# A five-place weight ring, and a second attention block whose next q, k, v and combinations are issued earlier

## The chip, the cores and the metric

One core of one Trainium2 chip (trn2) runs the whole kernel in one launch. The metric is the device time of an execution in microseconds. Engines are named TensorE (PE; PEld its weight loads), VectorE (DVE), ScalarE (ACT), GpSimd (POOL) and SyncE (SP, which issues most transfers).

## The reference, cut to what matters

Eight images of 16 x 16 tokens with 192 channels go through two blocks, each an attention and a mixture of experts (MoE). The norms are layer norms without weights, except `rms_norm`.

```
x = x + neighbourhood_attention(ln(x))            # 12 heads of 16, 7 x 7 neighbours
t = t + moe0(ln(t))                               # 32 experts of width 464, each token to 6,
                                                  # at most 48 tokens an expert; shared part of width 928
x = x + window_attention(ln(x))                   # within each row of 16 tokens
def L1_ffn(u):                                    # u = ln(t)
    h = u + causal_attention(rms_norm(u) @ w_qkv) # 12 query, 3 key heads, rotary, 256 tokens an image
    m = rms_norm(h)
    return h + sum_of_2_of_16_experts(m)          # width 384
t = t + L1_ffn(ln(t))
```

The output is x after both blocks, 2048 tokens by 192.

## The kernel before, in words

The kernel keeps x in SBUF (`x_all`, two tiles of 128 tokens an image). Five engines run their own instruction streams, which meet in semaphores. Matmul results go to eight PSUM banks, S0, S1, T0, T1, O0, O1, M0, M1. There are five stages.

*Stage A* is a loop over the images: neighbourhood attention, routing of the first MoE and its shared part. The tokens' normalised rows go to DRAM (`rows0`); `onehot` and small matmuls (`slot_ids`) count which token fills which place of an expert. Every image also has SyncE fill an eighth of the DRAM table `sorted_x` with an empty row (line 858). At the end of image 7, `a_tail` (line 1177) waits for the shared part, adds it to x, adds the ids, and only then line 1269 casts them to integers for the gathers.

*Stage B* runs the 32 experts as 16 pairs, of 64 slots each, two pairs a turn, in eight turns. GpSimd gathers the rows of the 16 pairs by indirect DMA (line 949) and copies two pairs at a time into `xs` (`b_x`, line 953; ScalarE copies the first two); TensorE transposes them (`b_rows`, lines 717 and 719), multiplies by gate and up weights (`b_gate_up`, lines 1690 and 1695), transposes the product, and multiplies by the down weights (line 1718); VectorE weighs the output (line 1292) and splits it into three bf16 parts, `y0_all`, whose sum is the f32 value. Weights of two pairs have a place (`RING = 2`); a refill waits for `b_gu` (gate and up used) or `b_y` (down used).

*Stage C*, the second block, combines the experts' outputs: for an image, `c_onehot` on GpSimd makes 32 bf16 matrices of 128 x 128 (`comb_s`, line 972), and TensorE multiplies them with `y0_all` (`c_comb`, line 1736) for each tile of tokens in a bank of its own. Its prologue combines image 0 and runs its window attention; then a loop over the images (`c_body`) does: add the window projection to x; normalise (statistics on VectorE, inverse root on GpSimd, lines 923 and 924, apply at line 809); root mean square norm (squares on ScalarE, another root on GpSimd); transposes (line 730); causal q, k, v (line 1761); rotation and the split into bf16 parts (`split_qk`); transposes of q and k (line 509); causal attention; projection (line 615); the second norm into `m_row`; then the window attention of the *next* image, with the router's steps of this one between its groups. The next image's combination is in two halves, one for each tile of tokens, one at the turn's start and one behind the causal q, k, v; its normalising and its q, k, v (`next_qkv`, lines 744 and 751) stand between the first two groups of scores of causal attention.

Attention works in groups `u`: scores (a mask matmul, line 535, then the heads, line 538) into a score bank; VectorE the negated maximum (line 651); ScalarE the exponentials (line 680); TensorE transposes of the probabilities (line 555); VectorE and ScalarE in turn the copies (lines 624 and 689); TensorE the weighting of v (line 573), `late` groups behind; at the end denominators (line 581), division on VectorE (641, 642), transposes (603), a copy (695) and the projection (615). `extra`, `between` and `before` are tables of steps which other parts of the kernel put between the groups. Each engine's order is the order written, so whatever stands in such a table delays what is behind it on that engine.

*Stage D* sorts tokens by expert into 48 tiles and runs the second MoE (`f_` functions, lines 1811 to 1837) with weights in a ring of six; the last stage adds its rows to x.

## Time and profile before

| | us |
|---|---|
| median of 3 runs | 1372.81 (1372.27 to 1373.34) |
| the profiled execution | 1371.57 |
| its span, first to last instruction | 1369.7 |
| TensorE busy in the span | 1081.2 (79%) |
| VectorE busy | 756.1 (55%) |
| ScalarE busy | 488.2 (36%) |
| GpSimd busy | 351.6 (26%) |
| mean granted clock of TensorE | 0.91 of full |

Busy time is a share of the whole span; no engine is busy throughout, and each stage has a limit of its own. A timeline row gives start and length in us, engine, line, what it writes and reads, how many instructions it merges, and in brackets the engine's idle time before it and who ended it.

### The profile page before, as it was taken

The numbers are of one execution on the slowest core, as the hardware profiler recorded it, in microseconds if no ns is written. First come the engines' busy times: TensorE is split into PE (matmuls) and PEld (weight loads), VectorE is DVE, ScalarE is ACT, GpSimd is POOL, SyncE is SP. The second block draws the span as 40 slices with busy tenths as digits, with TensorE's granted clock in tenths as the row PEclk, the third lists the DMA queues.
The fourth block names the chain that finished last, engine by engine and source line by source line (L and its number), as shares of the span: only waits on it lengthen the run. The fifth ranks groups of instructions, "written<-read, shape, count | busy, mean of one in ns | idle before, by whom it ended". The sixth has DMA issues, their size and how long they took to land.

```text
span 1369.7 us, 27161 instructions
## 1 busy us (share of the span) xinstructions
PE 1081.2 (79%) x9278; PEld 811.8 (59%) x9317; DVE 756.1 (55%) x2331; ACT 488.2 (36%) x1212; POOL 351.6 (26%) x588
## 2 busy tenths in 40 slices
PE   4899999999984997687777777777777662989993
PEld 3677777667762444455555556555555442878883
DVE  6668667766740343466665666666656553232324
ACT  2355345335521231435352534343444440211210
POOL 0000000000004024552533425161616101223332
PEclk9999999999986999799988999999989775999997
DMA  9054224404437793000000000000000003788885
GB/s 339 2 131 130 65 65 130 127 12 121 130 110 187 283 396 144 0 17 1 15 0 15 0 15 0 15 0 15 0 15 0 10 7 116 273 279 276 310 290 177
DMA packets 69193, 144.58 MB, mean 106 GB/s; under 512 B 4961, under 2 KB 55425, under 8 KB 66849
## 3 DMA queue, kind: packets, MB, share of 16 engines
q1 hardware_dynamic: 64352, 132.76, 29.3%
q0 software_dynamic: 4800, 11.32, 2.6%
q8 instruction: 22, 0.36, 0.1%
q14 instruction: 19, 0.15, 0.0%
HBM read 97.22 MB, written 46.83 MB: 105 GB/s over the span
## 4 chain that ended last, share of the span: by engine, by line
PE 34%; issue 33%; DVE 15%; POOL 8%; ACT 6%; DMA 4%; POOLq 0%; DVEq 0%; ACTq 0%; SPq 0%
PE bank L1607 4%; PE bank L1736 3%; PE bank L555 3%; PE bank L615 3%; PE bank L1635 3%; PE bank L573 3%; DMA R<-in_ffn_gu 2%; PE bank L1761 2%; PE bank L744 2%; DVE neg_max L651 2%; POOL rstd L924 2%; PE bank L751 2%; POOL R L972 2%; DVE R L624 1%; POOL token_y L1016 1%
## 5 line engine op out<-in xcount | busy, mean ns | idle before, releaser
L680 ACT ACTIVATE R<-bank,neg_max 128x128 f32<-128x128 f32 (+2 forms) x576 | 186.7, 405 | 91.3 <-DVE neg_max L651 90.6
L972 POOL TENSOR_SCALAR R<-cf,ids_rel 128x128 bf16<-128x128 f32 x288 | 187.9, 668 | 0.1
L923 POOL TENSOR_TENSOR rstd<-mean_var,cf 128x2 f32<-128x2 f32 x32 | 6.2, 193 | 625.0 <-DVE mean_var L804 625.0
L651 DVE TENSOR_REDUCE neg_max<-bank 128x2 f32<-128x352 f32 (+2 forms) x216 | 129.8, 611 | 47.0 <-PE bank L538 38.7
L555 PE MATMUL bank<-cf,R 128*128 128x128 f32 x864 | 135.2, 280 | 23.6 <-ACT R L689 17.5
L555 PEld LDWEIGHTS bank<-cf,R 128*128 128x128 f32 x864 | 94.8, 142 | 40.7 <-ACT R L689 16.2
L702 ACT ACTIVATE R<-bank 128x1024 bf16<-128x1024 bf16 x72 | 69.4, 1017 | 110.3 <-PE bank L509 110.3
L1607 PE MATMUL bank<-R 64*116 64x256 f32 (+1 forms) x512 | 97.4, 398 | 0.0
L509 PE MATMUL bank<-cb,R 128*128 128x128 bf16 x1008 | 74.6, 245 | 20.7 <-DVE R L494 20.4
L1522 DVE TENSOR_TENSOR R<-R,bank 128x384 f32<-128x384 f32 x48 | 26.6, 554 | 115.2 <-ACT R L1112 112.6
L1821 PE MATMUL bank<-xsT,R 128*128 128x128 f32 x576 | 76.3, 286 | 17.0 <-DMA R<-in_ffn_w 15.7
L509 PEld LDWEIGHTS bank<-cb,R 128*128 128x128 bf16 x1008 | 71.4, 113 | 27.8 <-DVE R L494 18.2
L538 PE MATMUL bank<-R 128*128 128x128 bf16 (+2 forms) x576 | 76.5, 235 | 11.5 <-DVE R L711 5.2
L1821 PEld LDWEIGHTS bank<-xsT,R 128*128 128x128 f32 x576 | 70.4, 197 | 23.6 <-DMA R<-in_ffn_w 15.0
L1607 PEld LDWEIGHTS bank<-R 64*116 64x116 f32 (+1 forms) x512 | 65.2, 180 | 26.2 <-issue 16.4
L1736 PE MATMUL bank<-R 128*128 128x384 bf16 (+1 forms) x512 | 74.6, 311 | 2.6 <-DVE R L1301 2.6
L1112 ACT ACTIVATE R<-bank 128x384 f32<-128x384 f32 x48 | 23.5, 490 | 148.4 <-PE bank L1828 148.4
L535 PE MATMUL bank<-cb 128*128 128x352 bf16 (+1 forms) x177 | 61.7, 349 | 14.8 <-ACT R L702 8.6
L689 ACT ACTIVATE R<-bank 128x512 f32<-128x512 f32 (+2 forms) x152 | 64.2, 460 | 14.7 <-PE bank L555 14.7
L1736 PEld LDWEIGHTS bank<-R 128*128 128x128 bf16 x512 | 51.8, 107 | 26.7 <-issue 8.7
L538 PEld LDWEIGHTS bank<-R 128*128 128x128 bf16 x576 | 50.5, 98 | 22.9 <-issue 0.5
L573 PE MATMUL bank<-R 128*32 128x128 f32 x1152 | 50.2, 281 | 14.8 <-ACT R L689 14.8
(249 smaller groups left out, 2006.2 us busy)
## 6 DMA issues: line engine op xcount, KB each, us to landing
R<-in_ffn_w SPq DMA_DIRECT2D x48, 864.0 KB, 6.1
sorted_x<-cmp SPq DMA_DIRECT2D x8, 4128.0 KB, 16.8
R<-in_ffn_gu SPq DMA_DIRECT2D x16, 1392.0 KB, 7.9
R<-in_ffn_dn SPq DMA_DIRECT2D x16, 768.0 KB, 5.8
xs_words<-sorted_x SPq DMA_DIRECT2D x48, 129.0 KB, 2.8
R<-token_y SPq DMA_DIRECT2D x8, 384.0 KB, 6.3
rows<-R SPq DMA_DIRECT2D x8, 224.0 KB, 2.3
out_x<-x_all SPq DMA_DIRECT2D x16, 96.0 KB, 2.5
```

The source lines that it names most:

```text
L509: ins = nc.tensor.transpose(bank[:, :].bitcast(BF16)[:, (h * 2 + t) * P:(h * 2 + t + 1) * P], qk_parts[:, row, :, :].rearrange("p s e -> p ...
L538: ins = nc.tensor.matmul(bank[:, g * kw:(g + 1) * kw], q_ap(h, t), k_ap(a, h, k0, kw), start=False, stop=(g == len(heads) - 1))
L555: ins = nc.tensor.transpose(PT[u % 2][:, at + g * P:at + (g + 1) * P], probs[:, u % 3, g * kw + c0:g * kw + c0 + P], ident)
L573: ins = nc.tensor.matmul(OB[t][j * HV:(j + 1) * HV, col:col + P], v_ap(a, h, vt), probsT[:, u % 4, at + g * P:at + (g + 1) * P], start=(k ...
L651: nc.vector.tensor_reduce(neg_max[:, u % 4, 0:g], score_bank(a, u)[:, 0:g * kw].rearrange("p (g k) -> p g k", g=g), AX, ALU.max, negate=Tr ...
L680: ins = nc.scalar.activation(probs[:, u % 3, g * kw:(g + 1) * kw], score_bank(a, u)[:, g * kw:(g + 1) * kw], ACT.Exp, bias=neg_max[:, u % ...
L689: copies_pt(lambda dst, src: nc.scalar.activation(dst, src, ACT.Copy), a, v).then_inc(psem("pta"), 1)
L702: nc.scalar.activation(qkT[:, h0:h0 + heads, :].rearrange("p h t -> p (h t)"), bank[:, :].bitcast(BF16)[:, 0:heads * 256], ACT.Copy, scale ...
L972: ins = nc.gpsimd.tensor_scalar(comb_s[:, t, j, :], cst("iota_tok"), ids_rel[:, j:j + 1], None, ALU.is_equal)
L1607: ins = nc.tensor.matmul(GATE[g % 3][part][0:DP0, c * 256:(c + 1) * 256], wsgu[rows, 2 if k else part, at:at + DP0], xnT_all[rows, k, :], ...
L1736: ins = nc.tensor.matmul(COMB[t][:, 0:(k1 - k0) * C], comb_s[:, t, j, :], y0_all[:, j, k0:k1, :].rearrange("p s c -> p (s c)"), start=(j = ...
L1821: nc.tensor.matmul(GU[r][part][:, c * P:(c + 1) * P], w[:, part * FF + c * P:part * FF + (c + 1) * P], xsT[:, r, 0, :], start=(c == 0), st ...
```

## The change

It has four parts. (1) The ring of stage B has five places, laid over buffers that stage A has done with; each place is loaded when what lay there is released; each later refill waits for the same semaphores as before, five pairs on. Gathered rows are read where they land, each two pairs have a semaphore (`b_rows0` to `b_rows7`), the loops of B are written out, and image 7's ids are added before its shared part (which goes to M0). (2) In stage C the combination of image i + 2 is in M1 alone, in three matmuls of 192 columns a step, 8 of 32 steps at the start of turn i and 24 behind the causal q, k, v; images 0 and 1 are combined before the loop. (3) The next image's normalised rows are transposed in the previous window attention, and its q, k, v are multiplied right behind the window projection; VectorE reads them before it applies the norm. (4) All attentions use three score banks; logits and ranks lie elsewhere. In stage D four of the first row loads move behind weight loads.

```
-RING = 2
+RING = 5
...
-        PT, OB, COMB = [T0, T1], [O0, O1], [T0, M1]
-        def score_banks(a):
-            return [S0, S1, M0] if a is NEIGH else [S0, S1, M0, M1]
+        LOGITS = M1[:, 2 * C:2 * C + 2 * E1]
+        SCORE = [S0, S1, M0]
...
-                if u == 3 and routed is not None:
-                    pe.wait_ge(s("c_expl"), routed)
...
-                    if u == min(us[-1] + late, a.n + 2):
+                    if u == min(us[-1] + 2 + len(us), a.n + 2):
...
+            for j, ready in ((2, lambda: await_(sp, NEIGH, "proj", B - 1, 1)), (3, lambda: sp.wait_ge(s("a_h"), GP * B)),
+                             (4, lambda: sp.wait_ge(s("a_shared"), B))):
+                ready()
+                load_gate_up(j)
+                load_down(j)
+            for j0 in range(RING, NPAIR, 2):
+                last = min(j0 + 2, NPAIR)
+                for j in range(j0, last):
+                    sp.wait_ge(s(f"b_gu{(j - RING) % 2}"), 2 * ((j - RING) // 2) + 2)
+                    load_gate_up(j)
+                for j in range(j0, last):
+                    sp.wait_ge(s("b_y"), (j - RING) // 2 + 1)
+                    load_down(j)
...
-            for t in range(WRING):
+            for t in (0, 1):
                 load_rows(t, t)
-            for t in range(1, WRING):
+            for t in (1, 2):
+                load_weights(t, t)
...
-                    .then_inc(s("b_rows_first" if j < 2 else "b_rows_rest"), 16)
-            pool.wait_ge(s("b_rows_rest"), 16 * (NPAIR - 2))
-            with pool.Fori(1, NPAIR // 2) as jj:
-                pool.wait_ge(s("b_xT"), jj)
-                b_x(jj)
+                    .then_inc(s(f"b_rows{j // 2}"), 16)
+            pool.wait_ge(s("a_done"), B + 1)
...
+            for i in range(3):
+                if i:
+                    pool.wait_ge(s("c_comb"), 2 * i)
+                    c_root(link, "c_var", i, mv, EPS6)
                 for t in range(2):
+                    c_onehot(link, i, t)
...
                 c_scatter(i)
-                if more:
-                    pool.wait_ge(s("c_comb"), 2 * i + 4)
-                    c_root(link, "c_var", 2 * i + 3, mv, EPS6)
-                    c_onehot(link, i + 2)
+                if level == 2:
+                    c_root(link, "c_var", 2 * i + 4, mv, EPS6)
+                    pool.wait_ge(s("c_comb"), 2 * i + 6)
+                    c_onehot(link, i + 3, 0)
                 c_root(link, "c_ss", 2 * i + 2, ss, EPS6)
+                if level == 2:
+                    c_onehot(link, i + 3, 1)
...
                 ln_stats(link, i, s("c_var"))
-                dve.wait_ge(s("c_rstd"), 4 * i + 2)
+                if level:
+                    conv_qk_dve(dve, WINDOW, brow, i + 1)
+                dve.wait_ge(s("c_rstd"), 4 * i + (3 - short(i)))
                 link(ln_apply(u_sb, i))
...
-                if more:
-                    c_combine(link, i + 1)
                 run(qk_copies_dve(dve, CAUSAL, i))
+                if level:
+                    between.update(zip(range(2, 8), split_qk(WINDOW, i + 1, link)))
+                if level == 2:
+                    between[1] = lambda: c_combine(link, i + 2)
+                    between[8] = lambda: c_norm(i + 2, 4 * i + 5)
...
+            def c_comb(i, n0, n1):
+                for n in range(n0, n1):
+                    t, j = divmod(n, NPAIR)
+                    if j == 0:
+                        pe.wait_ge(s("c_onehot"), 2 * i + t + 1)
+                    for k in range(3):
+                        ins = nc.tensor.matmul(M1[:, t * C:(t + 1) * C], comb_s[:, t, j, :], y0_all[:, j, k, :],
+                                               start=(j == 0 and k == 0), stop=(j == NPAIR - 1 and k == 2))
...
+            attention_pe(pe, WINDOW, 0, {2: lambda: c_comb(1, 0, 2 * NPAIR), (WINDOW.n, "transposed"): lambda: c_head(2)})
...
+                if level:
+                    pe.wait_ge(s("c_slots"), i + 1)
+                    pe.wait_ge(s("c_xTc"), 3 * i + 2)
+                    conv_qk_pe(pe, WINDOW, headT, wqkv, i + 1)
+                    conv_v_pe(pe, WINDOW, headT, wqkv, i + 1)
+                if level == 2:
+                    c_comb(i + 2, 0, EARLY_COMB)
+                c_head(2 * i + (3 - short(i)), M0)
...
+                if level == 2:
+                    c_comb(i + 2, EARLY_COMB, 2 * NPAIR)
                 transpose_qk(pe, CAUSAL, i)
-                attention_pe(pe, CAUSAL, i, None, {1: next_qkv, 2: banks_read} if more else {})
+                attention_pe(pe, CAUSAL, i, {"weighted": lambda: transpose_qk(pe, WINDOW, i + 1, n1=4)} if level else {})
                 project(pe, CAUSAL, wof, i)
-                if more:
-                    transpose_qk(pe, WINDOW, i + 1)
+                if level:
+                    transpose_qk(pe, WINDOW, i + 1, n0=4)
```

`level` is 2 for images 0 to 5, 1 for image 6 and 0 for image 7. On VectorE two of the window copies (`qk_copies_dve`) run before the causal projection is awaited; on ScalarE one does, and the copy of the next image's transposed rows (`c_copy` into `headT`) is put before the last gathering of outputs. `EARLY_COMB` is 8. The window projection goes to T0 and the causal one to M0. The loads of stage C's weights stand behind the ring's loads.

## Rows read from the trace of the kernel before

**Rows 1.** The page's first line

```profile
span 1369.7 us, 27161 instructions
```

**Rows 2.** Timeline of VectorE, 408 to 418 us

```profile
407.97 0.69 DVE L1242 TENSOR_TENSOR R<-R,bank 116x512 f32<-116x512 f32 x1 [0.61 <-ACT R L1042]
...
416.37 0.56 DVE L1180 TENSOR_TENSOR x_all<-x_all,bank 128x384 f32<-128x384 f32 x1 [7.42 <-PE bank L1635]
...
417.70 0.17 DVE L1269 CAST ids_i<-ids_f 128x16 int32<-128x16 f32 x1
```

**Rows 3.** Timeline of TensorE, 424 to 447 us

```profile
424.39 0.45 PE L717 MATMUL bank<-cf,xs_words 128*128 128x128 f32 x1 [8.13 <-ACT xs_words L1055]
...
433.36 1.01 PE L1695 MATMUL bank<-R,xsT 64*64 64x464 f32 x8
446.67 0.48 PE L717 MATMUL bank<-cf,xs_words 128*128 128x128 f32 x1 [12.30 <-POOL xs_words L955]
```

**Rows 4.** Source view of line 1292: min/median/max ns, first and last start

```profile
L1292 DVE TENSOR_TENSOR y_f<-bank,wsl x8: 557/558/559, 453.9 to 530.1; 128x384 f32<-128x384 f32 x8
```

**Rows 5.** Windows view: busy us of PE to POOL, granted clock, DMA share, GB/s

```profile
456.00:524.00 68.00, 63.67 (x504) 32.00 (x500) 28.57 (x59) 20.67 (x30) 20.90 (x37) 1.00 0.99 402
```

**Rows 6.** Source view of line 1338, the first VectorE step of a turn

```profile
L1338 DVE TENSOR_TENSOR x_all<-x_all,bank x8: 553/554/556, 583.4 to 1085.8; 128x384 f32 x7, 128x384 f32<-128x384 f32 x1
```

**Rows 7.** Timeline of one turn of stage C, all engines

```profile
870.57 4.09 PE L1736 MATMUL bank<-R 128*128 128x384 bf16 x32
870.88 0.55 DVE L1338 TENSOR_TENSOR x_all<-x_all,bank 128x384 f32 x1 [1.50 <-PE bank L615]
...
873.45 0.67 DVE L809 TENSOR_SCALAR h_words<-x_all,mean_var,rstd 128x192 f32 x2 [1.08 <-POOL rstd L924]
...
876.96 0.68 PE L730 MATMUL bank<-cf,R 128*96 128x128 f32 x4 [2.31 <-DVE R L1349]
...
878.33 4.21 PE L1761 MATMUL bank<-wqkvf,R 96*128 96x288 f32 x8 [0.68 <-ACT R L735]
...
882.33 5.34 PE L1736 MATMUL bank<-R 128*128 128x384 bf16 x32
...
887.75 1.85 PE L509 MATMUL bank<-cb,R 128*128 128x128 bf16 x30
...
893.49 2.84 PE L744 MATMUL bank<-wqkv,R 96*128 96x384 f32 x8 [0.76 <-ACT R L735]
...
898.21 0.68 DVE L651 TENSOR_REDUCE neg_max<-bank 128x4 f32<-128x512 f32 x1
```

**Rows 8.** Windows view of the same turn's causal q, k, v

```profile
877.00:882.30 5.30, 4.62 (x12) 3.08 (x13) 1.54 (x7) 0.59 (x1) 3.42 (x4) 0.60 0.27 100
```

**Rows 9.** Timeline of TensorE, the end of causal attention

```profile
912.64 0.65 PE L573 MATMUL bank<-R,v_causal 128*32 128x128 f32 x16 [0.87 <-DVE R L624]
...
916.31 2.93 PE L615 MATMUL bank<-wof,R 96*128 96x192 f32 x8 [0.68 <-ACT R L695]
919.03 4.47 PE L509 MATMUL bank<-cb,R 128*128 128x128 bf16 x48
...
924.02 0.39 PE L538 MATMUL bank<-R 128*128 128x128 bf16 x4
```

**Rows 10.** Source view of line 949, gathers issued at 418 to 421 us

```profile
DMA to landing us min/median/max: 3.8/4.1/5.1
```

**Rows 11.** The same, gathers issued at 432 to 437 us

```profile
DMA to landing us min/median/max: 8.5/8.6/9.2
```

**Rows 12.** Source view of line 858 at 398.3 us, the last fill

```profile
DMA to landing us min/median/max: 16.6/16.6/16.6
```

**Rows 13.** Timeline of TensorE in the first window attention

```profile
568.28 0.66 PE L555 MATMUL bank<-cf,R 128*128 128x128 f32 x4 [1.64 <-ACT R L680]
```

**Rows 14.** Source view of line 972, image 1's one-hots on GpSimd

```profile
L972 POOL TENSOR_SCALAR R<-cf,ids_rel x32: 593/597/1717, 546.0 to 567.4; 128x128 bf16<-128x128 f32 x32
```

**Rows 15.** Timeline of TensorE at the start of stage D

```profile
1162.79 2.93 PE L1821 MATMUL bank<-xsT,R 128*128 128x128 f32 x12 [2.92 <-DMA R<-in_ffn_w]
```

More of the change, by code:

```diff
@@ L399, in build @@
             psem(n)
+        for n in ("qkv", "read"):
+            psem(n, CAUSAL)
         block = ctx.enter_context(nc.Block())
@@ L781, in turns, with turns_c, short @@
             body(n - 1, False)
+        def turns_c(eng, body):
+            with eng.Fori(0, B - 2) as i:
+                body(i, 2)
+            body(B - 2, 1)
+            body(B - 1, 0)
+        def short(i):
+            return 1 if isinstance(i, int) and i == B - 1 else 0
         def tile_x(i, t):
@@ L1065, in b_body, with c_copy, c_body @@
                 nc.scalar.activation(hTs[0:DP0, 0, :], PT[0][0:DP0, :], ACT.Copy).then_inc(s("b_hTc0"), 1)
-            turns(act, NPAIR // 2, b_body)
-            def c_copy(k):
+            for jj in range(NPAIR // 2):
+                b_body(jj, jj + 1 < NPAIR // 2)
+            def c_copy(k, dst=xnT, bank=M0):
                 act.wait_ge(s("c_xT"), k)
-                copy_pair(xnT).then_inc(s("c_xTc"), 1)
-            c_copy(1)
+                copy_pair(dst, bank).then_inc(s("c_xTc"), 1)
+            c_copy(1, headT, S0)
             run(qk_copies_act(act, WINDOW, 0))
-            attention_act(act, WINDOW, 0)
-            def c_body(i, more):
+            attention_act(act, WINDOW, 0, last=lambda: c_copy(2, headT, S0))
+            def c_body(i, level):
                 def squares(n):
@@ L1082, in squares @@
                     ins.then_inc(s("c_ss"), 1)
+                steps = qk_copies_act(act, WINDOW, i + 1) if level else []
                 squares(0)
-                c_copy(3 * i + 2)
+                c_copy(3 * i + (3 - short(i)))
                 run(qk_copies_act(act, CAUSAL, i))
-                attention_act(act, CAUSAL, i, {0: lambda: c_copy(3 * i + 3)} if more else {})
+                attention_act(act, CAUSAL, i)
+                run(steps[:1])
                 squares(1)
+                run(steps[1:2])
+                c_copy(3 * i + (4 - short(i)))
+                run(steps[2:])
                 def router():
@@ L1256, in a_body @@
                     link(nc.vector.tensor_tensor(before0[:, :], before0[:, :], mask_b[:, t, :], ALU.add))
-                if not more:
-                    a_tail(link, i)
-                elif not first:
+                if more and not first:
                     link.end()
@@ L1380, in c_body @@
-                if more:
-                    steps += split_qk(WINDOW, i + 1, link)
-                attention_dve(dve, CAUSAL, i, link, dict(zip(range(1, 9), steps)) if more else {})
+                between = {}
+                if level:
[3 more added lines that the diff above has]
+                    between[8] = lambda: c_norm(i + 2, 4 * i + 5)
+                attention_dve(dve, CAUSAL, i, link, between)
@@ L1384, in c_body @@
+                copies = qk_copies_dve(dve, WINDOW, i + 1) if level else []
+                run(copies[:2])
                 await_(dve, CAUSAL, "proj", i, 1)
-                link(nc.vector.tensor_tensor(u_sb[:, :, :], u_sb[:, :, :], two(M1[:, 0:2 * C]), ALU.add))
+                link(nc.vector.tensor_tensor(u_sb[:, :, :], u_sb[:, :, :], two(M0[:, 0:2 * C]), ALU.add))
                 nc.vector.memset(scratch[:, 13:14], 0.0).then_inc(s("c_u"), 1)
-                link(nc.vector.tensor_tensor(image_x(i), image_x(i), two(M1[:, 0:2 * C]), ALU.add))
@@ L1388, in c_body @@
-                if more:
-                    copies = qk_copies_dve(dve, WINDOW, i + 1)
-                    run(copies[:1])
+                link(nc.vector.tensor_tensor(image_x(i), image_x(i), two(M0[:, 0:2 * C]), ALU.add))
                 dve.wait_ge(s("scattered"), 64 * i + 64)
                 nc.vector.tensor_scalar(m_row[:, :, TOKC], m_row[:, :, TOKC], 2.0 * P, None, ALU.add)
-                rms(1, m_row, 4 * i + (5 if more else 4)).then_inc(s("c_mr"), 1)
-                if more:
-                    run(copies[1:])
+                rms(1, m_row, 4 * i + (6 - (level < 2) - short(i))).then_inc(s("c_mr"), 1)
@@ L1398, in highest_logit @@
+                run(copies[2:])
                 def highest_logit():
                     dve.wait_ge(s("c_logits"), i + 1)
[L1400 removed]
+                    nc.vector.tensor_reduce(wsum[:, :, 0], two(LOGITS), AX, ALU.max, negate=True)\
                         .then_inc(s("c_negmax"), 1)
@@ L1724, in b_body @@
                     b_gate_up(jj + 1)
-            turns(pe, NPAIR // 2, b_body)
+            for jj in range(NPAIR // 2):
+                b_body(jj, jj + 1 < NPAIR // 2)
             pe.wait_ge(s("b_done"), LINKS["B"] * (NPAIR // 2))
```

342 lines of the change are left out of this document (177 added, 165 removed).

## The prediction

> **What bounds the kernel now.** I read the page first, for the span, which the sum below is made against [rows 1]; then busy time by stretch; then, because no engine is busy throughout, the timelines of four places, each from the last instruction backwards to what it waited for.
>
> *The hand-over to the first experts.* VectorE ends its part of image 7 at 408.7 us, but slot numbers are cast only at 417.7, behind the 6.9 us shared down-projection [rows 2]. TensorE's first expert transpose is at 424.4 and its second at 446.7, after 12.3 us of idle [rows 3]: GpSimd copies no later pair before all 14 later gathers have landed (line 956). The first pair's output is read at 453.9, the eighth's at 530.1 [rows 4].
>
> *The expert stream.* From 456 to 524 us the DMA engines are 99% busy at 402 GB/s [rows 5]. A pair of experts is 2.21 MB, 5.5 us, so a turn of two costs 11.0; observed are (530.1 - 453.9)/7 = 10.9. Both the transfers and TensorE's chain are at that length.
>
> *The second block (stage C).* Seven turns from 583.4 to 1085.8 us, 71.8 each [rows 6]. In the turn from 870.88 [rows 7] the start is a chain of small steps (add, statistics, root, apply), during which TensorE combines half of the next image in 4.09 us and then idles 2.3 us until 876.96. Its clock then falls: the eight q, k, v matmuls of 288 columns take 4.21 us, and the granted clock is 0.60 there [rows 8]; eight of 384 columns take 2.84 at 893.49. From 887.75 to 916.31 is causal attention. From 898.21 to 912.6 VectorE works almost without a break and TensorE's last weighting waits for it [rows 7, 9]. So VectorE sets the length there, and the preparation of the next image at 891 to 897 (attention stands still) is paid in full.
>
> **The change, part by part.**
>
> *Earlier gathers.* ids are added before the shared down-projection ends: cast at about 409.7, 8 us sooner. A gather lands after 3.8 to 5.1 us alone and 8.5 to 9.2 beside weight loads [rows 10, 11]. The last zero fill, issued at 398.3, flies for 16.6 us, to 414.9 [rows 12], and the new loads of experts 2 and 3 stand behind it, so I take the long landing: the second gather, issued at 411.4, is there at 420. TensorE needs its down-projection (to 416.3) and x added (417.0) first, so it starts at 420 in place of 424.4; 417 is the lower bound. "Trainium Kernel Development and Optimization", Key Constraints, in the Trainium skill says that DMAs issued by SyncE and GpSimd run on the same 16 engines and interleave; the trace agrees, by those two landings.
>
> *One wait per pair, and rows read in place.* From the first transpose to the end of gate and up were 10.0 us (424.39 to 434.37), from the second transpose to the output's read 7.2 (446.67 to 453.9) [rows 3, 4]. With the 12.3 us of idle gone the first output is read at 420 + 10 + 7.2, less 1 us for ScalarE's copy of rows: 436, instead of 453.9.
>
> *Ring of five.* Experts 2, 3 and 4 are asked for at 399, 409 and 416 us, when image 7's row, gating and shared part release their places, and from then on the ring runs a turn and a half ahead, so no turn waits for a single refill. With 7 more turns of 10.9 the eighth is read at 512. The stream allows about 508: 14 pairs at 5.5 us from 415, with some 10 us for the gathers (my estimate, from their landings while little else was in flight), is 502, and about 6 of work after the last weights. I take 511, a gain of 19; bounds 24 (start at 417, all cover holds) and 10 (each refill late). The unrolled loops add no work of an engine. The three weight loads for the second block move behind the ring, to about 500, and are hidden until 511.
>
> *Before the second block's loop.* The first combination has 96 matmuls of 192 columns instead of 64 of 384 and 192. The columns are the same; a step of 576 took 4.09/16 = 0.256 us [rows 7]. "TensorE: Matmul & The Clock Gate", Back-to-back issue gap, in the Trainium skill gives 81 ns for matmuls of 128 columns and 131 ns for 512 in a stream with weight loads, so three short ones would cost more than a long and a short one: interpolated, an estimate of 0.27 against 0.20 us, 2 us more an image. The trace does not agree: its 0.256 is already what the columns take at 2.4 GHz (0.240) plus little. I take no change; by the page it would be 16 us more over all images. The second image's combination is now inside the first window attention: 32 x 0.256 = 8.2 us, of which the 1.6 us that TensorE waited there (568.28) are cover [rows 13]. With its VectorE step +8.
>
> *One root behind 32 one-hots.* GpSimd makes image 2's one-hots before the loop, and only after image 1's combination is added. Image 1's took 22 us (546.0 to 568) [rows 14]. The combination's end is C; VectorE adds it at C + 4, the root follows, the one-hots run from C + 6.5 to C + 28.5. The rest of attention is 583.4 - 568.3 = 15.1 [rows 6, 13] plus 1, so turn 0 wants its own root at C + 17.5 and gets it at C + 29.5 where it could use it at C + 19.5: 10 us. Everything of the turn stands behind that root. In later turns one half of 16 runs under attention and one after the second root, with 7 us or more to spare.
>
> *A steady turn.* (a) Start: VectorE reads two banks of q and k before it applies the first root. The second is ready 2.84 us after TensorE begins, so the apply moves from 2.57 to 3.45: +0.9. TensorE meanwhile does 4.3 us of q, k, v (V is half of 2.84) and 8 combination steps (2.0), which end before x is normalised at 7.0. The idle time is filled, so I take the full clock: 288 columns then cost 2.1 in place of 4.21, -2.1. Behind them stand 24 steps, 6.1 us, against VectorE's 7.1 us of rotation and splitting from the first bank: both end at 16.6 to 16.9; before, 16.87. So 0. (b) Causal attention: the maximum of group 2 began 10.5 us after the transposes (898.21); with no preparation between, it can after two copies, two maxima and the combination's add and statistics (1.5), at 5.6: -4.9. The 14.4 us behind it stay and get 0.7 for normalising and some gaps: -3.8. (c) 32 of 48 transposes move ahead of the last denominators, at 62 ns (30 in 1.85) to 93 ns (48 in 4.47), less 0.6 of idle there: +1.9. (d) The projection took 2.93 us, half speed by the row of 384 columns; perhaps full: -0.7. (e) Before scores stood 48 transposes and those of m_row, 4.8 us after the projection (924.02); now 16 stand, but m_row is due at 3.5 by the same chain of add, squares, root and apply as at the turn's start, less the statistics, so scores gain 0.6, exponentials, which lose two ScalarE copies before them, 1.2, and group 3 waits no more for the router: -1.5. Sum -4.1; bounds -5.5 and +3 (half clock in a). Three banks in place of four cost nothing: scores of group u wait for the exponentials of u - 3, for which TensorE's preceding transposes have already waited.
>
> *Seven turns*: turn 0 has -4 + 10 and, after 10 us idle, half clock: +9.5. Five turns -20. Turn 6 has no combination or normalising: -5. The last turn 0.
>
> *Stage D*: TensorE waited 2.9 us for the second weights at 1162.79 [rows 15]; issued four row loads earlier, they are there: -3.5 with the clock's gain.
>
> Sum: -19 + 8 + 9.5 - 20 - 5 - 3.5 = -30. The profiled execution took 1371.57 us (1369.7 of span and 1.9 around it), 1.2 below the median of three, so 1342 to 1343; I say 1342.
>
> **Rivals.** (1) *Clock as before*: q, k, v keep 4.21 us and end at 12.5. The second group of 16 steps took 5.34 us where the first took 4.09, so 5.6 of them ran at half rate (0.48 us a step); with as many again, 24 steps end at 19.9, not 16.9: +3 in six turns, 1360. For it: this turn and its clock [rows 8]. Against: TensorE had idled 2.3 us before the fall, and the change fills that. 0.15. (2) *Slower*: TensorE stays at half clock until the combination is through. Steps of 0.48 us, 24 of them behind 4.2, end at 24.1: +7.2 in six turns, 1385. It decides from 22.0 us of the turn on, where six turns lose the 31 us. Against it: in that second group the clock came back. 0.06. (3) *The ring brings little*: gathers and refills hold the stream up, the eighth output is at 521: 1352. 0.09. (4) *More*: attention in (b) ends as VectorE's work alone, (c) is hidden by a full clock, the root stall is 5 us: -2 in six turns and -5, 1325. 0.12. (5) The stated case, 1330 to 1354 by its own terms: 0.58.
>
> **Numbers.** A measurement of this kernel tells about 0.2%, 2.7 us. Slower is (2) but for its milder end: 0.05; within 0.2% are that end and the tail of (1) near 1370: 0.03; faster the rest: 0.92. Range 1320 to 1364: it takes in (1), (3), most of (4).
>
> **What would show it.** First output near 436 and eighth near 511; turn 0 with a wait of about 10 us for a root behind one-hots; later turns of 67 to 68 us; granted clock 1.0 at the causal q, k, v, in about 2.1 us; transposes of causal attention 17 us into the turn; no wait for the second weights in stage D. I would be wrong if the combination's three pieces cost more than their columns, or if TensorE's clock does not hold.

## The result, and the profile after

The changed kernel took 1319.76 us in the median of four runs (1314.41 to 1323.49), the kernel before beside it 1373.07 (1372.27 to 1373.38): a ratio of 0.961, with a 95% interval of 0.9585 to 0.9639. It is faster, by 53 us where 30 were forecast, and 0.24 us below the low end of the range. Later runs of it gave 1315.87 (0.958) and 1316.05 (0.959). The profiled execution took 1314.41, 5.35 under the median, so the stage times below add up to a little more than the median's gain.

Where the 57.1 us between the two profiled spans are, in us:

| part | before | after | change | forecast |
|---|---|---|---|---|
| start to the eighth expert output | 530.1 | 511.7 | -18.4 | -19 |
| from there to the first turn | 53.3 | 58.1 | +4.8 | +8 |
| turn 0 | 69.9 | 74.9 | +5.0 | +9.5 against the mean turn of 71.8, so 81.3 |
| turns 1 to 5 | 360.9 | 324.0 | -36.9 | -20 |
| turn 6 | 71.6 | 65.0 | -6.6 | -5 |
| turn 7 and stage D | 283.9 | 278.9 | -5.0 | -3.5 |

(Turn 1 of the kernel before is a long one, 75.9 us; against its mean turn of 71.8 turns 1 to 5 gained 35.0.)

The page's first line, and the source views of the line that reads an expert output and of the first VectorE step of a turn; they answer to [rows 1, 4, 6]:

```profile
span 1312.6 us, 27217 instructions
```

```profile
L1341 DVE TENSOR_TENSOR y_f<-bank,wsl x8: 557/558/559, 436.1 to 511.7; 128x384 f32<-128x384 f32 x8
...
L1388 DVE TENSOR_TENSOR x_all<-x_all,bank x8: 553/554/555, 569.8 to 1033.7; 128x384 f32 x6, 128x384 f32<-128x384 f32 x2
```

TensorE's first expert transpose (timeline; it answers to [rows 3]) waits for the second gather and starts at 420.5, the forecast's 420; the first output is at 436, the eighth at 512, both as forecast.

```profile
420.53 0.44 PE L739 MATMUL bank<-cf,R 128*128 128x128 f32 x1 [6.47 <-DMA R<-rows,ids_i]
```

TensorE's timeline of the turn that starts at 839.10, against [rows 7, 9]:

```profile
842.67 2.15 PE L1796 MATMUL bank<-R 128*128 128x192 bf16 x24
845.54 0.68 PE L752 MATMUL bank<-cf,R 128*96 128x128 f32 x4 [0.73 <-DVE R L1401]
846.91 2.21 PE L1826 MATMUL bank<-wqkvf,R 96*128 96x288 f32 x8 [0.68 <-ACT R L757]
848.95 6.11 PE L1796 MATMUL bank<-R 128*128 128x192 bf16 x72
...
875.44 1.96 PE L536 MATMUL bank<-cb,R 128*128 128x128 bf16 x32
...
879.61 1.57 PE L637 MATMUL bank<-wof,R 96*128 96x192 f32 x8 [0.68 <-ACT R L717]
881.01 1.06 PE L536 MATMUL bank<-cb,R 128*128 128x128 bf16 x16
884.75 1.10 PE L752 MATMUL bank<-cf,m_row 128*96 128x128 f32 x4 [2.68 <-DVE m_row L1401]
```

The causal q, k, v take 2.21 us, not 4.21; a combination step costs 6.11/24 = 0.255 us, as its columns; and the projection takes 1.57 us, not 2.93. The windows view shows the granted clock, of a turn of before and of two of after (columns as in [rows 5]):

```profile
870.90:942.60 71.70, 54.52 (x467) 39.65 (x471) 45.26 (x144) 30.43 (x82) 29.46 (x49) 0.90 0.02 7
```

```profile
839.10:904.00 64.90, 49.54 (x498) 38.36 (x501) 44.17 (x140) 30.59 (x82) 29.53 (x49) 0.97 0.02 8
968.70:1033.70 65.00, 43.63 (x397) 31.37 (x400) 41.69 (x131) 30.07 (x81) 6.87 (x11) 0.92 0.03 9
```

A granted clock of 0.50 is TensorE at 1.2 GHz (half clock below), 1.00 is 2.4 GHz. The turn of before has 13.7 us at half clock, in two stretches of 6.8 us of which these windows show most:

```profile
878.00:884.60 6.60, 6.27 (x18) 4.12 (x19) 3.47 (x15) 0.27 (x1) 2.73 (x3) 0.50 0.22 80
915.60:922.30 6.70, 6.02 (x40) 5.82 (x40) 2.21 (x7) 2.30 (x6) 0.91 (x2) 0.50 0.00 0
```

The first takes in the causal q, k, v, the second the projection and the 48 transposes behind it [rows 7, 9]. After, 3.4 us are left (884.7 to 888.1). Work on VectorE, ScalarE and GpSimd is the same to about 1 us. Turn 0 has its wait of 7.8 us for a root, and the one-hots before it took 18.9 us in place of the 22 of [rows 14] (timeline of VectorE):

```profile
581.20 0.67 DVE L845 TENSOR_SCALAR h_words<-x_all,mean_var,rstd 128x192 f32 x2 [7.77 <-POOL rstd L971]
```

### The profile page after: what moved, and what is told of

Read it like the earlier page. It is cut to its first block, busy times and chain, and to the rows that moved or that the text cites. A ratio compares the mean times of both kernels' runs of the same rounds, so it can differ in the third digit from the quotient of the medians.

```text
span 1312.6 us, 27217 instructions
## 1 busy us (share of the span) xinstructions
PE 1043.5 (80%) x9541; PEld 805.9 (61%) x9573; DVE 747.4 (57%) x2308; ACT 481.1 (37%) x1205; POOL 347.6 (26%) x581
## 4 chain that ended last, share of the span: by engine, by line
issue 33%; PE 27%; POOL 17%; DVE 12%; ACT 5%; DMA 5%; POOLq 1%; DVEq 0%; ACTq 0%; SPq 0%
POOL R L1010 10%; PE bank L1659 4%; DMA R<-in_ffn_gu 3%; PE bank L577 2%; PE bank L1687 2%; POOL rstd L971 2%; POOL sorted_x L1031 2%; PE bank L595 2%; DVE neg_max L673 2%; PE bank L637 2%; POOL token_y L1058 1%; ACT R L702 1%; PE bank L1796 1%; PE bank L536 1%; PE bank L1746 1%
## 5 line engine op out<-in xcount | busy, mean ns | idle before, releaser
L1882 PE MATMUL bank<-xsT,R 128*128 128x128 f32 x576 | 75.9, 285 | 13.1 <-DMA R<-in_ffn_w 11.4
L536 PE MATMUL bank<-cb,R 128*128 128x128 bf16 x1008 | 67.5, 230 | 21.8 <-DVE R L521 21.8
L560 PE MATMUL bank<-R 128*128 128x128 bf16 (+2 forms) x576 | 79.4, 243 | 5.3 <-issue 4.6
L536 PEld LDWEIGHTS bank<-cb,R 128*128 128x128 bf16 x1008 | 62.8, 104 | 28.7 <-DVE R L521 17.9
L1154 ACT ACTIVATE R<-bank 128x384 f32<-128x384 f32 x48 | 23.6, 491 | 142.6 <-PE bank L1889 142.6
L557 PE MATMUL bank<-cb 128*128 128x352 bf16 (+1 forms) x184 | 65.8, 357 | 3.6 <-ACT R L724 3.2
L1796 PE MATMUL bank<-R 128*128 128x192 bf16 x768 | 66.0, 247 | 2.6 <-DVE R L1350 2.6
L560 PEld LDWEIGHTS bank<-R 128*128 128x128 bf16 x576 | 53.0, 103 | 24.6 <-issue 3.6
L1796 PEld LDWEIGHTS bank<-R 128*128 128x128 bf16 x768 | 64.1, 98 | 4.9 <-DVE R L1350 3.0
```

The costliest lines, as they stand in the source:

```text
L536: ins = nc.tensor.transpose(bank[:, :].bitcast(BF16)[:, (h * 2 + t) * P:(h * 2 + t + 1) * P], qk_parts[:, row, :, :].rearrange("p s e -> p ...
L557: nc.tensor.matmul(bank[:, 0:len(heads) * kw], cstb("identb"), cstb(mname, moff, len(heads) * kw), start=True, stop=False)
L560: ins = nc.tensor.matmul(bank[:, g * kw:(g + 1) * kw], q_ap(h, t), k_ap(a, h, k0, kw), start=False, stop=(g == len(heads) - 1))
L1796: ins = nc.tensor.matmul(M1[:, t * C:(t + 1) * C], comb_s[:, t, j, :], y0_all[:, j, k, :], start=(j == 0 and k == 0), stop=(j == NPAIR - 1 ...
L1882: nc.tensor.matmul(GU[r][part][:, c * P:(c + 1) * P], w[:, part * FF + c * P:part * FF + (c + 1) * P], xsT[:, r, 0, :], start=(c == 0), st ...
```

## The experiments

The question was why a steady turn fell by 6.8 us (71.7 to 64.9) and not by 4.1. Theory A: a good part is TensorE's clock, far beyond the causal q, k, v for which the prediction counted it. Theory B: the order of the work alone. Edits are to the changed kernel unless said otherwise.

### The changed kernel again (two runs)

> The changed kernel once more, nothing edited. Its four times went from 1314.41 to 1323.49 us at mean granted clocks of 0.940 to 0.929, while four of the kernel before kept within 1.1 us. If the 9 us come from the place of half-clock stretches, the times spread over 1314 to 1324 again, the longer ones at the lower clock, and the profile differs from the first one in a few turns by 1 to 2 us each where the granted clock is low. If they come from transfers (rival), the difference stands in the first block, in the expert stages or in stage D (before 511.7 or after 1096.8 us) at the same clock. If it was chance of one chip (rival), all times agree within 1.5 us.

> The changed kernel, nothing edited, beside the other three. Its turns took 64.9 us in both profiles (3.4 us of half clock in each) and its times 1313.9 to 1323.5. If the times spread by the turns' clock, a longer execution shows turns above 64.9; if the spread stands in turn 0, turn 7 and stage D alone (rival), the steady turns are 64.9 again whatever the time. 1314 to 1323.

1315.87 us (1313.87 to 1316.86) and 1316.05 (1315.35 to 1319.17). The steady turns are 64.9 again in both profiles, with 3.4 us of half clock each; turn 0 took 75.3 and 74.7 and began at 572.1 and 572.7 (569.8 in the first), turn 7 and stage D together took 275.3 and 277.7 (278.9 in the first). So the spread is not in the steady turns; what of it could be profiled stands ahead of turn 0 and behind turn 6. No execution of 1323 us was profiled, so its cause stays open.

### The combination late

```
-EARLY_COMB = 8
+EARLY_COMB = 0
```

> All 32 steps of the combination behind the causal projection of a turn, none ahead of the transposes of its input. If columns are what counts and the 8 early steps fill a wait of TensorE, 8 steps of 0.255 us go onto the path: +2.0 us in each of the six turns with a combination, +12 us in all. If the early steps also hold the clock (rival), TensorE idles 2.9 us at the turn's start, the causal projection runs at 4.2 instead of 2.2 us and the steps behind it at half clock for a while: +4 to +6 us a turn, +24 to +36 us. If the attention behind it has slack on TensorE (rival), 0 to +0.5 us a turn.

1358.61 us (1350.24 to 1360.46), +43 against the changed kernel beside it: more than any case expected. TensorE's timeline and the window of one turn:

```profile
874.51 0.68 PE L752 MATMUL bank<-cf,R 128*96 128x128 f32 x4 [2.71 <-DVE R L1401]
875.88 3.65 PE L1824 MATMUL bank<-wqkvf,R 96*128 96x288 f32 x8 [0.68 <-ACT R L757]
879.31 8.37 PE L1796 MATMUL bank<-R 128*128 128x192 bf16 x96
```

```profile
866.20:937.90 71.70, 55.20 (x502) 41.72 (x502) 44.23 (x140) 30.56 (x82) 29.44 (x49) 0.90 0.02 7
```

With 2.7 us of idle at that place the turn is as long as before the change, and has the same 13.7 us at half clock. Two microseconds of work, moved, are worth the whole gain of a steady turn. That can be the clock or the order, hence the next run.

### Idle products in the place of the early steps

```
-EARLY_COMB = 8
+EARLY_COMB = 0
 ...
+for n in range(24):
+    nc.tensor.matmul(M1[:, 0:C], cstb("identb"), y0_all[:, n % NPAIR, 0, :], start=True, stop=True)
-c_comb(i + 2, 0, EARLY_COMB)
```

> As the run with the combination late (none of its 32 steps ahead of the transposes), but 24 products of 192 columns whose sum nobody reads stand in the place of its first 8 steps. A steady turn took 71.7 us with the combination late and 64.9 with 8 steps early. If TensorE's work at that place counts only because it keeps the clock up, a turn needs the 2.0 us of 8 steps more than the changed kernel and nothing else: 66.9 us, the causal projection at 2.2 us, 13 to 15 us more than the changed kernel in all (1328 to 1333). If it is the order of the real work that counts (rival), the products only add to the path: 71.7 us or more, 1358 and above.

1336.68 us (1336.02 to 1337.96). Turns of 67.7 to 68.6, so products whose sum nobody reads give back 3.1 to 4.0 of the 6.8 us. In the turn from 717.7 the transposes of causal q and k begin 1.9 us later than in the changed kernel (17.8 against 15.85 us into the turn): the eight steps, as theory A has it. It ends 3.7 later all the same, with half clock in its last 21 us (765.7 to 773, and from 783 on). The time lies 4 us above theory A's 1328 to 1333 and far from theory B's 1358, so the clock is the larger part and idle products hold it less well than early steps.

```profile
717.70:786.40 68.70, 55.21 (x526) 42.99 (x525) 44.24 (x141) 30.56 (x82) 29.45 (x49) 0.93 0.02 8
```

### One piece of the combination

Only the largest of the three bf16 pieces of the expert outputs is combined; the two smaller ones are left out.

```
-for k in range(3):
+for k in range(1):
```

> The combination multiplies only the first of the three pieces of the expert outputs (the two smaller ones are left out, so the sum is rounded to bf16): 32 products of 192 columns in place of 96, 5.4 us of TensorE less for each image at full clock. If the 24 steps behind the projection lie on the path of a steady turn, a turn gets 6.1 - 2.0 = 4.1 us shorter: -25 us in turns and -5 us in the head. If TensorE's busy time there is also what keeps the clock up (rival), the granted clock of the steady turns falls from 0.97 to about 0.90, and the transposes, scores and copies that follow take most of it back: 0 to -1.5 us a turn. If VectorE's rotary and split set the transposes' start (rival: the split ends at 854.89, the combination at 855.06, 0.2 us apart), a turn gains 0.2 us only and the whole -3 to -6 us, most of it in the head.

1319.82 us (1318.85 to 1320.87), 4 us more than the changed kernel, though each image has 5.4 us less work on TensorE. From the eighth expert output to turn 0 it takes 8 to 10 us less; the turns are longer:

```profile
634.90:700.10 65.20, 47.40 (x438) 34.44 (x437) 44.15 (x141) 30.39 (x82) 29.46 (x49) 0.95 0.02 8
700.10:768.50 68.40, 51.17 (x439) 38.04 (x438) 44.29 (x141) 30.88 (x82) 29.44 (x49) 0.88 0.02 8
```

Causal q, k, v are back at 4.2 us in both, and the transposes start at 17.2. VectorE's split now ends last there: TensorE waits 1.8 and 2.1 us for it. So in these turns the combination's 6 us are not on the path: they lie beside VectorE's work, and they hold the clock.

### The kernel before with idle products

```
 if more:
     c_comb(i + 1, 0)
+for n in range(24):
+    nc.tensor.matmul(S1[:, 0:C], cstb("identb"), y0_all[:, n % NPAIR, 0, :], start=True, stop=True)
```

> The kernel before, with 24 products of 192 columns that nobody reads put ahead of the transposes of the causal input in each turn, where TensorE waited 2.31 us for VectorE and the clock then was at half for 6.8 us. If work at that place keeps the clock up, the causal projection takes 2.2 instead of 4.2 us and the second half of the combination 4.1 instead of 5.3: 2.5 to 3.5 us a turn, eight turns, 1345 to 1353 us without any of the change; the clock would then be the better part of what the change gains in a steady turn. If the clock falls because of the low rate of the whole turn, not of this wait (rival), 0 to -0.5 us a turn: 1369 to 1373. If the products push the transposes (rival: they start 2.3 us before rms ends and take 2.0 to 4.0), 0 to +1.5 us a turn, up to 1385.

1365.66 us (1357.06 to 1374.27), a ratio of 0.992 (0.989 to 0.995): faster than before by adding work. Windows of four successive turns of one execution:

```profile
803.60:871.70 68.10, 51.20 (x496) 37.10 (x495) 45.02 (x144) 30.48 (x82) 29.48 (x49) 1.00 0.02 8
871.70:939.70 68.00, 51.24 (x495) 37.06 (x493) 44.93 (x144) 30.52 (x82) 29.77 (x49) 1.00 0.02 8
939.70:1011.30 71.60, 55.84 (x496) 40.37 (x494) 44.99 (x143) 30.59 (x82) 29.48 (x49) 0.90 0.02 7
1011.30:1085.30 74.00, 58.51 (x495) 42.07 (x493) 44.98 (x144) 30.65 (x82) 29.76 (x49) 0.85 0.02 7
```

The code of the turns is one loop, and VectorE, ScalarE and GpSimd are busy for the same time in each; only the clock differs. At full clock the old order takes 68.0 us (TensorE still waits 0.32 us behind the products, so they put nothing on its path). In that turn's timeline the old projection and transposes are at full speed too:

```profile
877.74 0.69 PE L730 MATMUL bank<-cf,R 128*96 128x128 f32 x4 [0.32 <-DVE R L1349]
879.10 2.21 PE L1763 MATMUL bank<-wqkvf,R 96*128 96x288 f32 x8 [0.68 <-ACT R L735]
...
915.31 1.57 PE L615 MATMUL bank<-wof,R 96*128 96x192 f32 x8 [0.68 <-ACT R L695]
916.71 2.85 PE L509 MATMUL bank<-cb,R 128*128 128x128 bf16 x48
920.40 0.68 PE L730 MATMUL bank<-cf,m_row 128*96 128x128 f32 x4 [0.84 <-DVE m_row L1349]
```

Against [rows 7, 9]: 2.21 for 4.21, 1.57 for 2.93, 2.85 for 4.47. With 32 products instead of 24:

> The kernel before with 32 idle products in place of 24 ahead of the causal input's transposes. With 24, three turns kept full clock at 68.0 us, the others took 71.7 to 73.9, and the times went from 1357 to 1374. If the share of the clock in a steady turn of the kernel before is 3.7 us, turns 2 to 6 take 68.0 to 68.7 (the 8 further products push the transposes by up to 0.7 us) and the whole 1350 to 1358. If 24 were already too many or the place is the wrong one for the other stretch (rival), the turns stay mixed: 1357 to 1374, as with 24.

1366.59 us (1356.94 to 1372.1): turns of 68.1 to 74.3 in one profile, mixed as with 24. One filled place does not secure the clock in the old order; where it holds, the turn is at 68 to 69.

### The transposes behind the projection

```
-attention_pe(pe, CAUSAL, i, {"weighted": lambda: transpose_qk(pe, WINDOW, i + 1, n1=4)} if level else {})
+attention_pe(pe, CAUSAL, i)
 project(pe, CAUSAL, wof, i)
-    transpose_qk(pe, WINDOW, i + 1, n0=4)
+    transpose_qk(pe, WINDOW, i + 1)
```

and their copies on ScalarE and VectorE behind the second squares and the second rms.

> The 32 transposes of the next image's q and k that stand ahead of the causal denominators go behind the projection, to the 16 that are there, and their copies on ScalarE and VectorE behind the second squares and the second rms. If they cost on the path what they take (1.96 us from 875.44 to 877.40), the projection comes 2.0 us earlier; the 48 transposes then take 3.2 us and end about as m_row is ready (PE waited 2.68 us there), so TensorE loses nothing, but the score products wait for the copies, which now end 1.5 to 2.5 us later: a turn changes by -0.5 to +1.0 us, the whole by -4 to +7. If the first products of the next attention hang on the copies alone (rival), +2.5 us a turn, +17. If the copies overlap the router's start (rival), -2 us a turn, -14. The half-clock stretch at 884.7 (3.4 us) should go where TensorE no longer idles there.

1335.55 us (1324.15 to 1340.31), +20, though in the profiled execution some turns are shorter than the changed kernel's 64.9:

```profile
648.50:716.80 68.30, 55.66 (x502) 42.74 (x502) 44.30 (x140) 30.55 (x82) 29.46 (x49) 0.90 0.02 8
785.10:851.00 65.90, 52.93 (x502) 39.46 (x502) 44.14 (x141) 30.60 (x82) 29.47 (x49) 0.95 0.02 8
851.00:914.80 63.80, 51.10 (x502) 38.84 (x501) 43.95 (x140) 30.60 (x82) 29.53 (x49) 0.97 0.02 8
```

At an equal clock of 0.97 the turn is 1.1 us shorter without the 32 transposes ahead of the denominators. Three of its five steady turns were at 65.8 or 68.3.

### Sixteen steps early, alone and with the transposes behind

> 16 in place of 8 of the combination's 32 steps ahead of the transposes. TensorE waited 0.73 us there in the changed kernel, so 8 more steps (2.0 us) push the transposes by 1.3 us and free 2.0 us behind the projection, where the combination and VectorE's split ended within 0.2 us of each other: the split, which starts from the projection, would now end 1.3 us later: +1.3 us in six turns, +8 us. If the combination's end is the bound (rival), -0.7 us a turn, -4 us. If the clock is now less at risk (rival), the times spread less, within 2 us, at +0 to +8.

`EARLY_COMB = 16`: 1317.07 us (1314.37 to 1320.55), no difference from 8. A steady turn has no half clock left and is as long as before:

```profile
841.90:906.80 64.90, 49.16 (x502) 37.34 (x501) 44.10 (x140) 30.44 (x82) 29.48 (x49) 1.00 0.02 8
```

Its transposes start at 16.8 us in place of 15.85, and the router's part at full clock gives the 1 us back. So the 3.4 us of half clock at 884.7 cost the changed kernel about 1 us a turn. Two later runs show the same directly. They change only when SyncE issues loads outside stage C (the last section of the experiments), and in each of them turn 1, with the code of the changed kernel, ran wholly at full clock and took 63.9 us; here it is in the run with the old load times of the ring:

```profile
652.40:716.30 63.90, 49.24 (x503) 37.31 (x502) 44.13 (x141) 30.44 (x82) 29.50 (x49) 1.00 0.02 8
```

> All 48 window transposes behind the projection, as before, and 16 in place of 8 steps of the combination early. With 8 steps the turns with 3.4 us of half clock took 63.8, those with 13.7 us 68.3; 16 steps early left no half clock in a steady turn of the changed kernel (64.9). If early work holds the clock here too, the turns take 63.5 to 64.0 and the whole is 4 to 8 us under the changed kernel run beside it, 1308 to 1313. If the clock is lost in the attention for want of the transposes there (rival), turns of 68.3 stay in some executions: 1320 to 1340. If the 16 steps cost on this path (rival), 64.9: no change.

1323.45 us (1320.12 to 1324.76), turns of 65.3 to 67.3: the clock is still lost in some.

> As the run with the transposes behind and 16 steps early, and 24 idle products behind the transposes, where TensorE waits for m_row. If TensorE's wait there is what the half-clock stretch around the end of the causal part follows, no turn has one and each takes 63.0 to 63.8: 1306 to 1311. If the products reach past m_row (rival: 48 transposes and 24 products take 5.0 us, the wait was 2.7 + 2.0 us long), the router's transposes come 0.3 to 1 us later: 64.5, 1312 to 1317. If the clock falls in the attentions all the same (rival), as the run without the products.

1319.22 us (1317.57 to 1337.18). Once the clock is held for whole turns they take 64.8, with 23.6 us from the first causal transposes to the projection (24.7 in the changed kernel, 28.6 before). None of the three beats the changed kernel.

### The root of turn 0, and the last two turns

```
-for t in range(2):
+for t in range(2 if i < 2 else 1):
     c_onehot(link, i, t)
 ...
 c_root(link, "c_ss", 2 * i + 1, ss, EPS6)
+if first:
+    c_onehot(link, 2, 1)
```

> GpSimd compares the second half of image 2's one-hots (9.3 us) behind turn 0's first two roots in place of ahead of them. Turn 0 of the changed kernel: VectorE waits 7.8 us for the first root behind 18.9 us of one-hots. If that wait is what makes the turn 74.9 us long, TensorE's causal products start 7.8 us earlier and the second half of the combination then waits for the one-hots, which end some 3 us after it would have started: turn 0 gets 5 to 7 us shorter (68 to 70 us) and the whole 5 to 7 us. If the clock goes with it (rival): TensorE now waits in the middle of the combination, the clock falls there, and only 1 to 3 us are left. If the wait only moves (rival: the combination waits as long as VectorE did), 0 to 1 us.

1315.82 us (1314.53 to 1318.09), turn 0 at 74.8: no gain. The wait moved, to TensorE (timeline):

```profile
580.45 2.21 PE L1829 MATMUL bank<-wqkvf,R 96*128 96x288 f32 x8 [0.68 <-ACT R L757]
582.49 2.15 PE L1799 MATMUL bank<-R 128*128 128x192 bf16 x24
589.55 5.79 PE L1799 MATMUL bank<-R 128*128 128x192 bf16 x48 [4.91 <-POOL R L1010]
```

The transposes behind it begin 23.3 us into the turn in place of 26.9, yet the turn has 16.8 us at half clock in place of 11.1 and gives the 3.6 us back.

> The changed kernel, and in turns 6 and 7, which have no combination, 24 products nobody reads at its place. Turn 6 took 65.0 us with 10.2 us of half clock at its start, though it has 6 us less on TensorE than a steady turn. If idle time there drops the clock, as in the run with the combination late, the products give back 1.4 us on the causal projection, 1 us on the transposes behind it and some on the next stretches: turn 6 at 61 to 63 us, turn 7 1 to 2 us shorter, 3 to 6 us in all. If 2 us of products cannot hold the clock where no combination follows (rival), turn 6 and 7 take 0 to 2 us more each. If those turns hang on VectorE alone there (rival), 0.

The same 24 idle products in turns 6 and 7: 1316.23 us (1312.87 to 1319.89), turn 6 at 64.7 with 10.2 us of half clock, as without them. They do not hold the clock there, and nothing is gained.

### The ring, the gathers, and stage D

> The changed kernel, but the loads of expert pairs 2 to 8 of the first block's experts start as in the kernel before: gate and up when the pair before has been multiplied, down when its output is there, none before the shared part of the last image is added. If the gain of stage B (first output 436 after 454 us, last 511.7 after 530.1) comes from weights that travel during the end of the first block and beside the gathers, the first output stays near 436 (its weights were in place), the second waits for its pair until 450 to 455, and the outputs follow at 10.5 us or a little more: last at 525 to 530, +13 to +18 us in all. If the gain comes from the earlier identifiers and the gathers waited for pair by pair, and the traffic has its old pace anyway (rival), the last output comes at 512 to 516: 0 to +4 us. If two buffers also leave the queue empty between pairs (rival), 12 us or more from output to output: last at 536, +24.

The loads of pairs 2 and on wait as with two buffers: 1323.08 us (1320.96 to 1328.14).

> TensorE waits for all 16 gathers before its first expert rows instead of for the first two. The first two landed at 420.5 us, the last ones about 10 us later. If the outputs are bound by the weights, which flow at 0.99 of the transfer engines' time, the first outputs come 8 to 10 us later, but the buffers of five hide it: the last output at 512 to 516, 0 to +4 us. If the chain from output to output is TensorE's and VectorE's (rival), the whole stage moves: last output at 520 to 522, +8 to +10 us.

TensorE waits for all 16 gathers first: 1341.30 us (1338.95 to 1342.33). Source views of the read output, first with the old load times, then with all gathers; and TensorE's first expert transpose in the latter:

```profile
L1336 DVE TENSOR_TENSOR y_f<-bank,wsl x8: 557/558/559, 432.7 to 516.4; 128x384 f32<-128x384 f32 x8
```

```profile
L1341 DVE TENSOR_TENSOR y_f<-bank,wsl x8: 557/558/559, 461.8 to 534.9; 128x384 f32<-128x384 f32 x8
```

```profile
446.53 0.45 PE L739 MATMUL bank<-cf,R 128*128 128x128 f32 x1 [28.93 <-DMA R<-rows,ids_i]
```

The early loads of a ring of five bring 3 to 5 us at the last output (511.7 to 513.3 in three profiles against 516.4). They also slow the first gathers: without them TensorE's first expert transpose is at 417.4, not 420.5 to 423.2. One wait for each pair brings 22: beside the weights the last gather lands at 446.5, where the kernel before also made its second expert transpose [rows 3]. The five buffers hide none of it, for from 438 to 504 us TensorE is busy 62 of 66 us; both it and the transfers (share 1.00, 398 GB/s) are nearly always busy. The slot numbers were not cast at the same time in all profiles (409.4 to 411.6 us in three of the changed kernel, 409.1 and 413.0 in these two); counted from the cast, the loads are worth 5 to 7 us and the waits 20 to 22.

> Stage D's first loads in the order of the kernel before: the rows of six tiles, then the weights of five. Stage D took 220.6 us before, 215.8 and 212 in two profiles of the changed kernel. If the order is what made it shorter, it returns to 219 to 221: +4 us. If the earlier scatter and the removed waits did it (rival), 0 to +1 us. If it is the spread of stage D between executions (rival), no shift beyond that spread of 4 us.

Rows first in stage D: 1323.09 us (1319.76 to 1328.12), a ratio of 0.965 (0.962 to 0.969) against 0.958 (0.956 to 0.960) on another chip for the changed kernel; turn 7 and stage D took 280.9 us where three profiles of the changed kernel had 275.3 to 278.9. By the total alone that is hardly beyond the spread. The timeline of TensorE at the start of stage D is plainer, in the changed kernel and then with rows first:

```profile
1105.00 5.32 PE L1882 MATMUL bank<-xsT,R 128*128 128x128 f32 x24 [0.47 <-ACT xsT L1149]
```

```profile
1106.89 2.78 PE L1875 MATMUL bank<-xsT,R 128*128 128x128 f32 x12 [0.47 <-ACT xsT L1142]
1112.38 2.57 PE L1875 MATMUL bank<-xsT,R 128*128 128x128 f32 x12 [2.71 <-DMA R<-in_ffn_w]
```

With rows first the wait for the second weights is back (2.71 us; 2.92 in [rows 15]), and all three profiles of the changed kernel are without it. From the first transposes of stage D to the end of these 24 products it took 9.7 us with rows first, and 5.8 to 6.9 in the changed kernel. So the order removes that wait, and is worth 2.8 to 3.9 us there.

## Why the prediction was right and wrong

**Right.** The first experts: start 420, outputs 436 and 512, for the named reasons. The share it gave the ring was too large, though: refills that all come late were to cost 9 us of the gain of 19, and the old load times cost 3 to 5 (5 to 7 from the cast); the wait for each pair carries the gain. The combination's three pieces cost their columns (0.255 us a step). Turn 0 is 10.1 us longer than the turns behind it: its norm is applied 8.4 us later, for the root behind the one-hots, the half clock after that wait costs 2.7, and 1.0 comes back at its end. From the eighth output to turn 0, +8 was +4.8 to +6.8. In stage D the wait for the second weights is gone, as forecast; turn 7 and stage D together gained 5.0 to 8.6 us in three profiles, where -3.5 was forecast, and no run shows where the rest of that comes from.

**The step that failed** is the size of *five steady turns at -4.1*, which were -6.8 to -7.0 each, some 15 us in all, and the same error in turns 0 and 6 (3 us and 2 us). Turn 0 was overpriced twice more: 10 us for the root, where 8.4 came, and 3.5 for half clock, where 2.7 less 1.0 came. Term by term, in us a turn; the fourth column compares the two orders with both at full clock, the old one in the kernel before with idle products (68.0 us) and the new one in the turn of 63.9:

| term | forecast | measured | both at full clock | measured from |
|---|---|---|---|---|
| (a) start to causal transposes | 0 | -1.0 | +0.4 | 15.85 against 16.87 into the turn |
| (b) causal attention | -3.8 | -5.0 | -4.6 | 23.6 (transposes behind) against 28.6 |
| (c) 32 transposes moved ahead | +1.9 | +1.1 | +1.1 | 24.7 against 23.6 |
| (d) projection | -0.7 | -1.4 | 0 | 1.57 against 2.93 |
| (e) after the projection | -1.5 | -0.5 | -1.0 | 22.9 against 23.3, from its end to the turn's |
| sum | -4.1 | -6.8 | -4.1 | |

The working priced (a) with TensorE at full clock, and from there on went by rows of the kernel before (0.062 to 0.093 us a transpose, "the 14.4 us behind it stay", half of the projection's gain) which hold the second stretch at half clock. Its own condition, that filled idle time keeps the clock, was not carried through to that stretch. Of the 6.8 us, 4.1 are the order of the work (68.0 less 63.9) and 2.7 the clock: half clock cost the old turn 3.7 us (71.7 less 68.0) and still costs the new one 1.0, behind the projection. That the order alone comes to the forecast's -4.1 is luck: the forecast's sum held 0.7 us of clock in (d), and its other four terms were off by 0.4 to 0.8 us, in both directions. In (a) the norm was applied 2.9 us into the turn and not 3.45. In (e) TensorE now waits 2.68 us for m_row, where it transposed before. Rival (4) had the effects that came, a shorter (b) and a (c) at full clock, and was given 12% and 2 us a turn for them; the low end should have carried full clock through the whole turn, 3.7 us in seven turns.

**The rivals.** (1), clock as before, did not come with 8 early steps; it is what the kernel is with none (71.7 us a turn, 1358.6), so the gain of a steady turn stood on two microseconds of matmuls at one place. (2), slower, and (3), the eighth output at 521, did not come.

## What to carry to other kernels

Before costing a turn from the rows of a trace, mark which rows ran at half clock, and price each at both levels: when a change fills one wait of TensorE, every later stretch of the loop may move too. Removing TensorE work, or moving it away from a wait, can cost more than it saves (5.4 us less work an image: +4 us; eight steps moved: +43 us). In a stream of experts look first at the wait for small gathers that share the transfer engines with the weights: splitting it was worth 22 us here, the earlier loads of deeper buffers 3 to 5.

## What the runs showed of the hardware

The same loop body took 68.0, 71.6 and 74.0 us in successive turns of one execution, at granted clocks of 1.00, 0.90 and 0.85, with every other engine equally busy. At the place where the clock was lost or held, TensorE waited 2.3 us in the kernel before and 2.7 with the combination late, with 0.7 us more one step later. "TensorE: Matmul & The Clock Gate", HAM oscillation, in the Trainium skill names idle time between groups of matmuls, repeated in each pass of a loop, as what takes the clock away; the trace agrees with that in kind. No run here shows what exactly the fall depends on, and 24 idle products that held the clock in a steady turn of one kernel did not hold it in turn 6 of another.
